# Graph attention turned around: score tiles with destinations on the partitions, transposed by TensorE

## The reference

```
h = x @ W                                        # (625, heads, c)
e = leaky_relu(al_s[src] + al_d[dst], 0.2)       # al_s, al_d: one number per node and head
a = exp(e - segment_max(e, dst));  a = a / (segment_sum(a, dst) + 1e-16)
out[dst] += h[src] * a                           # then bias, and what the layer has behind it
```

## Time and profile before

| | us |
|---|---|
| median of 3 runs | 1633.42 (1632.71 to 1636.35) |
| the profiled execution, its own time | 1632.61 |
| span of its profile | 1630.9 |
| TensorE matmul busy | 1451.2 (89%) |
| VectorE busy | 818.5 (50%) |
| ScalarE busy | 428.6 (26%) |
| GpSimd busy | 501.0 (31%) |

### The profile page before, as it was taken

How to read it: one execution, slowest core, us unless ns; L and a number is a source line. 1 busy time by engine, 2 the same in 40 slices (tenths; PEclk the granted TensorE clock), 3 DMA queues, 4 the chain that set the end, 5 groups by cost and what they waited for, 6 DMA issues and landing times.

```text
span 1630.9 us, 23173 instructions
## 1 busy us (share of the span) xinstructions
PE 1451.2 (89%) x8170; PEld 1341.1 (82%) x8170; DVE 818.5 (50%) x1883; ACT 428.6 (26%) x766; POOL 501.0 (31%) x570
## 2 busy tenths in 40 slices
PE   5898799999999999999999998997599949877884
PEld 3566699999999999999998897986489728877762
DVE  7889544224534465642233354138731362798433
ACT  1153511111010101101012214254322423666221
POOL 5111323342424443344334222343222650200110
PEclk9999799999999999999999998999799979988887
DMA  3110111212442242422112112220022200100001
GB/s 115 37 30 21 29 40 32 57 45 73 107 134 75 88 113 79 129 68 59 36 52 74 33 39 80 78 75 8 1 68 63 63 1 25 34 1 1 10 1 47
DMA packets 57524, 86.52 MB, mean 53 GB/s; under 512 B 6437, under 2 KB 54053, under 8 KB 57303
## 3 DMA queue, kind: packets, MB, share of 16 engines
q1 hardware_dynamic: 45184, 66.02, 13.9%
q10 hardware_dynamic: 12244, 19.17, 4.0%
HBM read 83.24 MB, written 1.92 MB: 52 GB/s over the span
## 4 chain that ended last, share of the span: by engine, by line
PE 74%; DVE 18%; issue 3%; ACT 3%; DMA 1%; POOL 0%; DVEq 0%; ACTq 0%; SPq 0%
PE psum L1788 12%; PE psum L1791 12%; PE psum L1792 12%; PE psum L1805 7%; PE psum L1808 7%; PE psum L2225 6%; PE psum L2122 3%; PE psum L2126 3%; PE psum L2127 3%; PE psum L2138 2%; PE psum L1893 2%; DVE max_scratch L1582 2%; DVE ln_stats L1260 2%; DVE probs L1606 2%; PE psum L1777 1%
## 5 line engine op out<-in xcount | busy, mean ns | idle before, releaser
L1788 PE MATMUL psum<-w_lo,xT_hi 128*125 128x384 f32 (+1 forms) x1110 | 382.7, 345 | 6.8 <-ACT packed_sums L735 3.2
L1791 PE MATMUL psum<-w_hi,xT_lo 128*125 128x384 f32 (+1 forms) x1110 | 378.3, 341 | 0.0
L1792 PE MATMUL psum<-w_hi,xT_hi 128*125 128x384 f32 (+1 forms) x1110 | 377.6, 340 | 0.0
L665 POOL CAST w_hi<-w_raw 128x384 fp32r<-128x384 f32 x190 | 103.4, 544 | 504.6 <-PE psum L1792 493.8
L678 POOL TENSOR_TENSOR w_lo<-w_raw,w_hi 128x384 fp32r<-128x384 f32 x106 | 114.7, 1113 | 454.2 <-ACT w_hi L905 344.9
L1166 DVE TENSOR_TENSOR h_lo<-psum,h_hi 125x384 fp32r<-125x384 f32 (+1 forms) x120 | 66.9, 557 | 317.4 <-ACT h_hi L763 316.4
L1788 PEld LDWEIGHTS psum<-w_lo,xT_hi 128*125 128x125 f32 (+1 forms) x1110 | 209.1, 188 | 9.1 <-ACT packed_sums L735 3.7
L1791 PEld LDWEIGHTS psum<-w_hi,xT_lo 128*125 128x125 f32 (+1 forms) x1110 | 209.4, 189 | 0.1
L1792 PEld LDWEIGHTS psum<-w_hi,xT_hi 128*125 128x125 f32 (+1 forms) x1110 | 209.0, 188 | 0.0
L667 POOL TENSOR_TENSOR w_lo<-w_raw,w_hi 128x384 fp32r<-128x384 f32 x190 | 200.8, 1057 | 15.2
L1805 PE MATMUL psum<-h_lo,adjacency 125*125 125x384 f32 (+3 forms) x600 | 203.6, 339 | 1.9 <-ACT adjacency L803 1.7
(11 more groups left out here) (275 smaller groups left out, 2168.0 us busy)
## 6 DMA issues: line engine op xcount, KB each, us to landing
w_raw<-weights_dram SPq DMA_DIRECT2D x296, 192.0 KB, 2.4
score_w_raw<-weights_dram ACTq DMA_DIRECT2D x58, 192.0 KB, 2.9
x_nat<-x_dram SPq DMA_DIRECT2D x1, 1875.0 KB
x_residual<-x_dram SPq DMA_DIRECT2D x1, 1875.0 KB
out_dram<-x_residual SPq DMA_DIRECT2D x5, 375.0 KB
score_a_rows<-L_gnn_a_src_dram ACTq DMA_DIRECT2D x8, 192.0 KB, 3.6
score_a_rows<-L_gnn_a_dst_dram ACTq DMA_DIRECT2D x8, 192.0 KB, 5.0
rgcn_bias<-rgcn_bias_dram SPq DMA_DIRECT2D x1, 1125.0 KB
```

What stands on the lines that cost most here:

```text
L665: nc.gpsimd.tensor_copy(mem.wh[:, slot, :], mem.raw[:, raw_slot, :]).then_inc(w_hi_ready, 1)
L1788: ins = nc.tensor.matmul(o, h, wl, start=(j == 0), stop=False, skip_group_check=True)
L1791: nc.tensor.matmul(o, l, wh, start=False, stop=False, skip_group_check=True)
L1792: ins = nc.tensor.matmul(o, h, wh, start=False, stop=stop and j == k - 1, skip_group_check=True)
```

## The change

All four layers get a new form of the scores.

- **Tiles.** A tile j belongs to a head h and a destination block b. Its 125 partitions are destinations, its 625 columns all the sources. In Q0, Q1 and Q3 b is the outer loop and h the inner; in Q2 (`by_head`) h stays outer.
- **Rows.** Only one row per head is spread (`send_row`: 2 pieces, 512 and 113 columns wide, in place of 36 small matmuls). ScalarE keeps it times 0.8 (`keep_row`); `largest` and `columns` stay as they are but always read PSUM. The two numbers per destination are now per partition.
- **`steep_or_flat`**, VectorE: kept row plus one per-partition number, then max with another, 125 x 625, SBUF to SBUF (one `tensor_scalar`).
- **`turn_tile`**, TensorE: five 125 x 125 transposes into PSUM, four blocks to a bank (a "turn"), a ring of three or four banks.
- **`exps`**, ScalarE: one exp per 125 x 125 block, in place in PSUM, with a per-partition bias. The tile's other exp is gone.
- **`probs`**, VectorE: min with 1, times the counts, from PSUM, in parts that do not cross a turn (`parts`: eight per four tiles).
- **`sum_tile`**, TensorE: the same matmuls as before, now five in a row into one bank for one destination block, so that block is complete when its last tile is.
- **Behind it.** `out_scaled` on ScalarE (Q0, Q1) scales the block by the inverse sum as it is read; bias is added to `features` beforehand on GpSimd (`feature_bias`); statistics, norm, gain, ReLU, skip and the transposes of the next input for a finished block are written between the tiles of the next blocks. In Q0 the square roots of one block so stand between the exps of others. In Q2 `head_read`, `elu_exp`, `head_elu` handle one head of all five blocks at a time. `early_scores` stands one or two products later.

The diff, cut to its core:

```diff
+        if self.by_head:
+            self.tiles = [(h, b) for h in range(heads) for b in range(NB)]
+        else:
+            self.tiles = [(h, b) for b in range(NB) for h in range(heads)]
...
+Q0 = Attention(None, HEADS2, C2, KC, PIECES1, True, BASE_L2, True,
+               {13: (0,), 16: (1,), 19: (2,), 22: (3,)}, {26: 0, 27: 1, 28: 2},
+               {2: ((0, 1), 0), 3: ((2, 3), 0), 4: ((), 3)})
+Q1 = Attention(Q0, 1, D, K8, PIECES, True, BASE_L2B, True,
+               {9: (0,)}, {13: 0, 14: 1, 15: 2, 17: 3, 18: 4},
+               {1: ((0,), 3), 2: ((), NB)})
+Q2 = Attention(Q1, HEADS3, C3, KC, PIECES, False, BASE_L3, False,
+               {1: (0,), 4: (1,)}, {}, {0: ((0, 1), 0)})
+Q3 = Attention(Q2, 1, D, KC, PIECES, False, BASE_L3 + 2 * KC, False,
+               {1: (0,)}, {}, {0: ((0,), 0)})
...
+            def q0_gain(b):
+                pool.wait_ge(normed[2], b + 1)
...
+            for j in range(len(Q0.tiles)):
+                split_to(min(Q0.end + 2 + 2 * max(0, j - 3), Q0.end + AHEAD))
+                if j in (3, 7):
+                    q0_residual(j // 4 + 1)
+                if j >= 11 and (j - 11) % 4 == 0:
+                    q0_gain((j - 11) // 4)
...
+            def keep_row(q, h):
+                act.wait_ge(row_sent, q.head0 + h + 1)
+                if h >= 4:
+                    act.wait_ge(g_ready, q.tile0 + (h - 3) * NB)
+                a = row_col(q)
+                nc.scalar.activation(kept_row(q, h), ps[0:BP, a:a + N], ACT.Copy, scale=1.0 - SLOPE).then_inc(row_kept, 1)
...
+            def exps(q, tiles):
+                for v in range(exps_made[q.index], q.turns_within(tiles)):
+                    act.wait_ge(g_turned, q.blocks_of_turn(v))
+                    last = min(4 * v + 4, len(q.tiles) * NB)
+                    for n in range(4 * v, last):
+                        h, b = q.tiles[n // NB]
+                        t = turned_part(q, v, n, n + 1)
+                        ins = nc.scalar.activation(t, t, ACT.Exp, bias=mem.al_src2[0:BP, n % NB, h:h + 1])
+                    ins.then_inc(exp_done, 1)
...
-                def exps(j):
-                    h, k = j // NB, j % NB
...
-                    nc.scalar.activation(mem.score[0:BP, j % 3, :], mem.rows[0:BP, h % 2, 0:N], ACT.Exp,
-                                         bias=mem.al[0:BP, k, h:h + 1]).then_inc(exp_done, 1)
-                    if j >= 2:
-                        act.wait_ge(top_ready, q.head0 * NB + j - 1)
-                    nc.scalar.activation(flat[0:BP, j % 2, :], mem.rows[0:BP, h % 2, N:2 * N], ACT.Exp,
-                                         bias=mem.al_src2[0:BP, k, h:h + 1]).then_inc(exp_done, 1)
...
+            def out_scaled(q, u, dest):
...
+                nc.scalar.activation(dest, bank(q.out_bank(u), 0, width), ACT.Copy, scale=z).then_inc(part_read, 1)
...
+            for j in range(4 * NB + 7):
+                if j < 4 * NB:
+                    q0_read(j)
+                if j + 4 <= 4 * NB:
+                    exps(Q0, j + 4)
+                if j < 4:
+                    split_hi(Q0.end + 2 * j + 3)
+                b = (j - 4) // 4
+                if j % 4 == 0 and 0 <= b < NB:
+                    std(2)(b)
+                if j % 4 == 1 and 0 <= b < NB:
+                    norm(2, dest0, dest0)(b)
...
+            def probs(q, tiles):
...
+                end = [i for i, part in enumerate(q.parts) if part[0] < q.turns_within(tiles)][-1] + 1
+                for v, j, c0, c1 in q.parts[parts_made[q.index]:end]:
+                    h, b = q.tiles[j]
+                    dve.wait_ge(exp_done, q.turn0 + v + 1)
...
-                def tops(j):
-
-                    dve.wait_ge(exp_done, 2 * (P0 + j + 1))
-                    t = mem.score[0:BP, j % 3, :]
-                    nc.vector.scalar_tensor_tensor(t, t, 1.0, flat[0:BP, j % 2, :], ALU.min, ALU.max
-                                                   ).then_inc(top_ready, 1)
...
+            def steep_or_flat(q, j):
+                h, b = q.tiles[j]
+                dve.wait_ge(cols_ready, q.head0 + h + 1)
+                dve.wait_ge(row_kept, q.head0 + h + 1)
+                if j >= q.g_ring:
+                    dve.wait_ge(g_turned, (q.tile0 + j - q.g_ring + 1) * NB)
+                nc.vector.tensor_scalar(g_tile(q, j), kept_row(q, h), mem.row1[0:BP, b, h:h + 1], mem.row2[0:BP, b, h:h + 1],
+                                        ALU.add, ALU.max).then_inc(g_ready, 1)
+            scores_begin(Q0)
...
+            for j in range(4 * NB + 7):
+                if j + 3 < 4 * NB:
+                    steep_or_flat(Q0, j + 3)
+                if j < 4 * NB:
+                    h, b = Q0.tiles[j]
+                    dve.wait_ge(part_done, j + 1)
+                    inverse(mem.z[0:BP, b, h:h + 1], bank(Q0.out_bank(j), C2, C2 + 1), False).then_inc(z_ready, 1)
+                if j + 3 <= 4 * NB:
+                    probs(Q0, j + 3)
+                b = (j - 2) // 4
+                if j % 4 == 2 and 0 <= b < NB:
+                    q0_stat(b, 0)
+                b = (j - 4) // 4
+                if j % 4 == 0 and 0 <= b < NB:
+                    link(q0_stat(b, 1))
+                    var(2, b)
+                if j % 4 == 1 and 0 <= b < NB:
+                    shift(2)(b)
...
+                if j % 4 == 3 and 0 <= b < NB:
+                    q0_out(b)
...
+            def q1_out(b):
+                t = x_res(b)
+                dve.wait_ge(gained, NB + b + 1)
+                link(nc.vector.tensor_tensor(t, t, mem.resid[0:BP, b, 0:D], ALU.add))
...
+            for s in range(NB + 2):
+                if s < NB:
+                    dve.wait_ge(part_done, Q1.unit0 + 2 * s + 1)
+                    inverse(mem.z[0:BP, s, 0:1], bank(Q1.out_bank(2 * s), HW, HW + 1), False).then_inc(z_ready, 1)
+                    q1_stat(s, 0)
+                if 0 <= s - 2 < NB:
+                    turn_lo(T_Q[2], KC, mem.xh, mem.xl, False, s - 2)
+                if 0 <= s - 1 < NB:
+                    q1_out(s - 1)
+                    shift(4)(s - 1)
+                if s < NB:
+                    link(q1_stat(s, 1))
...
+            def head_read(h):
...
+                link(inverse(z, head_out(h)[:, :, C3], True))
+                t = strip(h)
+                nc.vector.tensor_tensor(t, head_out(h)[:, :, 0:C3], mem.z[0:BP, :, h % 2:h % 2 + 1].to_broadcast([BP, NB, C3]),
+                                        ALU.mult).then_inc(part_read, 1)
+                dve.wait_ge(part_read, Q2.unit0 + h + 1)
+                b = mem.par[1][0:BP, h * C3:(h + 1) * C3].rearrange("p (a c) -> p a c", a=1).to_broadcast([BP, NB, C3])
+                nc.vector.tensor_tensor(t, t, b, ALU.add).then_inc(elu_in, 1)
...
+            def head_elu(h):
...
                 link(nc.vector.tensor_scalar(e, e, 1.0, -1.0, ALU.min, ALU.add))
                 nc.vector.scalar_tensor_tensor(t, t, 0.0, e, ALU.max, ALU.add).then_inc(layer_ready, 1)
...
+            for j in range(len(Q2.tiles)):
+                h, b = Q2.tiles[j]
+                if j + 3 < len(Q2.tiles):
+                    steep_or_flat(Q2, j + 3)
+                probs(Q2, j + 1)
+                if h + 2 < Q2.heads and b:
+                    largest(Q2, h + 2, b - 1)
+                    if b == NB - 1:
+                        largest(Q2, h + 2, b)
+                        columns(Q2, h + 2)
+                if b == 2 and h:
+                    head_read(h - 1)
+                if b == NB - 1 and h:
+                    head_elu(h - 1)
...
+            for s in range(NB):
+                dve.wait_ge(part_done, Q3.unit0 + 2 * s + 1)
+                link(inverse(mem.z[0:BP, s, 0:1], bank(Q3.out_bank(2 * s), HW, HW + 1), True))
+                last_half(s, 0)
+                if s:
+                    shift(5)(s - 1)
+                link(last_half(s, 1))
+                var(5, s)
...
+            def send_row(q, h):
...
+                w = 2 * q.heads
+                for p, e, a, z in score_pieces(row_col(q)):
+                    ins = nc.tensor.matmul(ps[0:BP, p:e], mem.ident[0:w, h:h + 1].to_broadcast([w, BP]),
+                                           mem.al_T[0:w, a:z], start=True, stop=True)
+                ins.then_inc(row_sent, 1)
...
+            def turn_tile(q, j):
+                pe.wait_ge(g_ready, q.tile0 + j + 1)
...
+                    nc.tensor.transpose(turned_part(q, v, n, n + 1), g_tile(q, j)[:, nodes(c)], mem.ident[0:BP, 0:BP]
+                                        ).then_inc(g_turned, 1)
...
+            def sum_unit(q, j, u):
...
+                for k in range(NB):
+                    ins = nc.tensor.matmul(bank(q.out_bank(u), off, off + width), blocks(p_tile(q, j))[:, k, :],
+                                           feat_flat(q, k, a, a + width), start=(k == 0 and off == 0),
+                                           stop=(k == NB - 1), skip_group_check=True)
...
+            for j in range(4 * NB):
```

(65 more changed lines are left out.)

870 lines of the change are left out of this document (467 added, 403 removed).

## The result

The changed kernel takes 1625.84 us (median of 5 runs, 1625.38 to 1628.28), the kernel before 1634.02 in the same rounds: ratio 0.995, 95% interval 0.9939 to 0.9962. It is 0.5% faster, where I had forecast 4.6%, and the time lies 27 us above my range. The profiled execution took 1625.7 us, 1.7 of them outside its span.

The account below looks back on a forecast made before the run. TensorE was taken to bound products and the sums of Q1 and Q3, VectorE Q2's sums, Q0's mixed, with 89.0 us of gaps. Terms sum to -74.9: 1632.6 to 1557.7, plus 0.8 for the median, 1559 us; range 1536 to 1599.

Parts of the forecast that it names:

- Q0, "3.1 us per tile", 70 us: Q0's sums: TensorE's hand-over and ScalarE's list each 3.1 us per tile, taken as 3.4; 70 us for 66.3 (+4).
- Q2, "13.9 us per head", 107.5 us: Q2's sums: VectorE's work 13.9 us for six heads, 11 for the last two; 107.5 us for 110.1 (-2.6).
- Q1's products, "no change": Q1's product stretch: TensorE's own, 99.17 of 99.9 us busy; foreseen to stay at 99.9 us.
- my upper bound: Whole kernel, 1599 us: rival (A) 21, ScalarE's exps at 0.385 (11 in Q0), 8 of waits in product stretches.
- Q3's sums, -1.3: Q3's sums: 35.9 to 34.6 us, -1.3.
- Q2's products, -3: Q2's product stretch: two heads' small matmuls become two rows, and no slow start; -3 us.
- Q1's round: Q1's sums and gap: one block per round, a chain through all queues of 8.9 us; 45 for 63.1, -18 us.
- the end, 11.9 for 9.5: Kernel's end: four output DMAs out early, one block's norm chain 3.7 us and DMA 5.8; 9.5 for 22.6, -13.1 us.
- Q3's products, -9.3: Q3's product stretch: rows stay away, scores come after the products as one 4 us hand-over; 46 for 55.3, -9.3 us.
- (A): Rival, chance 0.16: VectorE and GpSimd block each other, `steep_or_flat` suffers in Q0 or runs slower; 21 us, so 1580.
- (B): Rival, chance 0.09: table exchanges lie on Q0's path, seven more loads of 1.28 us; 14 us with what follows, so 1573.
- (C): Rival, chance 0.05: slower, the four-engine hand-over does not overlap; +104 us in Q2, +43 in Q0, so 1705.

Follow-up runs that it names:

- run 9: Changed kernel with only Q0's x8 units moved: second unit turned two tiles after the first, ScalarE's x8T_hi one tile ahead of VectorE's x8T_lo; 1612.26 us.
- run 5: The kernel of the four moves: changed kernel with Q0's x8 units, Q2's row, the weight splits (4 ahead at two pieces) and Q3's probs moved; 1581.95 us.
- run 10: Changed kernel with only Q2's row of head h+3 sent ahead of the last sum of head h; 1612.04 us.
- runs 3: Changed kernel with ScalarE splitting 4 chunks ahead, not 8, before reading a piece's banks, except at Q1's piece 1; 1623.48 us.
- run 4: Changed kernel with Q3's probs made for three tiles ahead of VectorE's first read, the rest between the reads; 1621.98 us.
- run 6: Run 5's kernel with GpSimd's gain of Q0's normalisation done on 8 of its 1024 columns; 1575.08 us.
- run 7: Run 5's kernel with ScalarE's square root in Q0's normalisation replaced by a copy, so no table is exchanged; 1572.57 us.
- the first trials of two moves: Each alone on the changed kernel: Q0's second x8 unit one tile later on three engines, 1624.51 us; Q2's row behind the previous head's last sum, 1621.71 us.

## Why the prediction was wrong

The sign was right, and most prices; two steps of the sum failed above all, by the same fault: a stage was taken as long as its fullest engine is busy.

- **Q0, "3.1 us per tile", 70 us.** Wrong. I set one tile's sum and its hand-over from VectorE, 3.1 us, beside ScalarE's list for a block, 12.4 us or 3.1 a tile, and took 3.4. ScalarE's list is a sum of busy times, and the chain of the x8 units (turn, x8T_hi, x8T_lo, turn of the next unit) was in the sum only as ScalarE's 0.6 us each; it was never laid along the orders of the three engines: it begins on TensorE in one tile's round and must be back in the next, while ScalarE has a table load, exps and a normalisation queued in between. It cost 14.1 us of waits in three places, and half clock behind them (behind the 5.14 us wait a tile's ten sum matmuls took 3.52 us, at full clock 2.33). Shown: moving both ends of that chain alone gives 15.7 us back (run 9), the split at the last piece 3.3 more (run 5), and Q0 stands at 74.7, for 71.5 foreseen.
- **Q2, "13.9 us per head", 107.5 us.** The same: VectorE's 13.9 was right (13.5 busy), and assumed that it never waits. `largest` waits for a row that TensorE sends behind the head's first sum, 2.9 to 3.4 us a head. Shown: with the row ahead of the last sum, 130.4 becomes 115.6 (run 10). The 8 us that remain in run 10 lie almost wholly at the start of the stage: the first sum begins 6.5 us behind the products, where I had put 2, and the first head takes 17.3 us; the next five take 14.1 each, for 13.9 foreseen, and the last two 21.2 together, for 22. That start in run 10:

```profile
1395.10 1.28 ACT L1059 ACT_TABLE_LOAD   x1
...
1398.98 2.42 PE L2420 MATMUL psum<-features,more_tiles 125*125 125x97 f32 x10 [4.31 <-DVE more_tiles L1794]
```

The table load lies ahead of the first exps, and the row for the third head is sent behind the first sum. What each of the two costs there was not tried.
- **Q1's products, "no change".** Wrong by 9.7. I had named weight splits in that stretch in my upper bound, at 8 us, for GpSimd's biases between them, so the size was foreseen but kept out of the sum. It is ScalarE, told to split eight chunks ahead before it reads a full bank, that waits for loads which GpSimd's pace releases. Shown by runs 3 and 5: 99.2 us, with GpSimd's biases left where they were.
- **Q3's sums, -1.3.** +5.7 instead: five tiles of probs stand before the first read in VectorE's order. Shown by run 4; 36.6 with it mended.
- **Q2's products, -3, and Q1's round.** +2.4 instead: 2.27 us of wait for w_lo behind `keep_row`. Not tried apart. Q1's sums and gap, 48.3 for 45.1, and the end, 11.9 for 9.5, are sizes: the round in Q1, 8.9 us foreseen, took 10.0 (the transposes of the finished blocks begin at 1313.54, 1323.46, 1333.49 and 1343.51 us).
- **Q3's products, -9.3,** were better than I took, 40.5 for 46: 5.5 us that hide as much of the other misses.

**The rivals.** (A) was a real mechanism. Both engines around one `steep_or_flat`, which should take 0.60 us:

```profile
1123.67 2.69 DVE L1829 TENSOR_SCALAR score_tiles<-score_tiles,row_steep,row_flat 125x625 f32<-125x625 f32 x1
1123.68 2.34 POOL L777 TENSOR_TENSOR dest_even<-dest_even,par 125x1024 f32<-125x1024 f32 x1 [8.05 <-ACT dest_even L1004]
...
1126.42 1.06 PE L2407 MATMUL psum<-ident,score_tiles 125*125 125x125 f32 x5 [2.77 <-DVE score_tiles L1829]
```

VectorE's ends 0.34 us behind GpSimd's. The Trainium skill (SBUF — State Buffer, SBUF: two separate sides) calls the pair of ports between the two an exclusive lock that is held for the whole instruction; the trace agrees. I had put (A) at 21 us. Over all 66 `steep_or_flat` behind 1093 us the excess is about 5 us (44.7 us of busy time, less 66 times 0.60), and leaving GpSimd's gain out gives 4.8 us in Q0 (run 6), the gain's own place in the chain included. (B) is 4.9 us (run 7), not 14; the stage has seven loads, for one before. Both were priced on the kernel of the four moves, which is 44 us shorter; on the changed kernel neither was tried. Other places of (A) are not priced at all: at the end of Q3's products the four instructions of `columns` took 7.1 us together, about 0.7 elsewhere, beside GpSimd's additions. (C) gave the sign of the surprise but not its kind. A tile in Q2 takes 3.26 us (130.4/40), 0.6 over the 2.69 of my sum and over the 3 us that I had named as a sign of being wrong; one in Q0 takes 4.7, 1.1 over the 3.58 of my sum. The hand-over overlaps in most tiles; it stops at one fixed place per block and head. None of my cases held "one instruction out of place in an otherwise sound order", and so my range had no room for it.

## What to carry to other kernels

A stage's time on several in-order engines is not the busy time of the fullest one. For every wait that an engine executes, write down what the releasing engine has queued ahead of the release, and whether the waiter's own queue holds work that others need; do this for the rare steps (once per block or head) as for the inner loop, since here four of them cost 44 us of a foreseen 75. And when a wait is mended at one end, ask at once who stands at the other: in their stages the first trials of two moves gave 3.8 and 4.2 us, the moves carried through 15.7 and 14.8.
